# A gather in two halves, three tiled turns in place of four, and loads waited for in groups

## The reference

```python
def reference(x, itok_B_1_198, L0_cond_weights):
    # x: (64, 64, 512) float32; itok: (64,) int32; weights: (200, 64, 64) float32
    w = L0_cond_weights[itok_B_1_198]                    # (64, 64, 64): one 64 x 64 matrix for each sample
    return x + jnp.einsum('bct,bcd->bdt', x, w)
```

## Time and profile before

| | us |
|---|---|
| median of 3 runs | 47.34 (47.32 to 47.43) |
| the profiled execution | 47.17 |
| its span, from the first to the last instruction | 45.3 |
| TensorE busy | 24.1 |
| VectorE busy | 14.8 |
| ScalarE busy | 13.9 |
| moved by DMA | 17.83 MB, mean 394 GB/s |

### The profile page before, as it was taken

One profiled execution on the slowest core, in us unless ns is written; L12 is line 12 of the kernel. 1 busy time (PEld: TensorE's weight loads), 2 busy tenths in 40 slices (PEclk: granted clock), 3 DMA queues, 4 the chain that ended last, 5 costly groups with the idle time before them and its releaser, 6 DMA issues.

```text
span 45.3 us, 305 instructions
## 1 busy us (share of the span) xinstructions
PE 24.1 (53%) x98; PEld 10.0 (22%) x98; DVE 14.8 (33%) x24; ACT 13.9 (31%) x16; POOL 1.6 (4%) x9
## 2 busy tenths in 40 slices
PE   0040000000000099999999999999999999700000
PEld 0040000000000042233454335445344344000000
DVE  1310000000039930067599960280280286140000
ACT  0899100000000050067589840260260265130000
POOL 4009000000000000000000000000000000000000
PEclk9999999999999999999999999999999999999997
DMA  0589999999999999999999999999999999999990
GB/s 0 109 333 434 413 427 427 442 405 434 449 413 427 434 420 427 427 420 427 427 420 427 427 427 420 427 427 420 434 449 391 449 434 413 427 434 384 431 395 22
DMA packets 2594, 17.83 MB, mean 394 GB/s; under 512 B 290, under 2 KB 290, under 8 KB 546
## 3 DMA queue, kind: packets, MB, share of 16 engines
q1 hardware_dynamic: 2448, 16.78, 88.9%
q0 software_dynamic: 144, 1.05, 5.5%
q10 hardware_dynamic: 2, 0.00, 0.0%
HBM read 9.44 MB, written 8.39 MB: 394 GB/s over the span
## 4 chain that ended last, share of the span: by engine, by line
PE 52%; DMA 21%; DVE 7%; issue 5%; POOL 1%; POOLq 1%; DVEq 0%
PE product L148 31%; DMA gathered<-weights,table_row 21%; PE product L152 21%; DVE w_all L179 5%; DVE y_sb L192 2%; POOL piece L124 1%; DVE gathered L176 1%; POOLq L33 1%; DVEq L173 0%; POOLq L201 0%
## 5 line engine op out<-in xcount | busy, mean ns | idle before, releaser
L152 PE MATMUL product<-x_sb,w_all 64*64 64x512 f32 x64 | 9.6, 760 | 12.9 <-DVE w_all L179 12.9
L148 PE MATMUL product<-x_sb,w_diag 128*128 128x512 f32 x32 | 14.0, 595 | 0.0
L188 DVE COPY y_sb<-product 128x1024 f32<-128x1024 f32 x7 | 8.6, 1225 | 11.1 <-PE product L148 6.8
L114 ACT COPY y_sb<-product 128x1024 f32<-128x1024 f32 x7 | 7.1, 1013 | 11.8 <-PE product L148 7.4
L148 PEld LDWEIGHTS product<-x_sb,w_diag 128*128 128x128 f32 x32 | 6.0, 190 | 7.9 <-issue 7.9
L152 PEld LDWEIGHTS product<-x_sb,w_all 64*64 64x64 f32 x64 | 3.5, 209 | 18.3 <-DVE w_all L179 13.0
L110 ACT COPY w_diag<-w_all 64x256 f32<-64x256 f32 x4 | 2.5, 636 | 11.2 <-DVE w_all L179 11.2
L176 DVE TENSOR_TENSOR gathered<-gathered,piece 128x64 f32<-128x64 f32 x1 | 0.3, 270 | 10.0 <-DMA gathered<-weights,table_row 10.0
L179 DVE STREAM_TRANSPOSE w_all<-gathered 128x2048 f32<-128x2048 f32 x1 | 2.3, 2311 | 0.0
L105 ACT COPY w_diag<-zero 64x1024 f32<-64x1024 f32 x2 | 2.1, 1042 | 0.0
L192 DVE COPY y_sb<-product 128x512 f32<-128x512 f32 x2 | 1.4, 692 | 1.5 <-PE product L148 1.5
(11 more groups left out here) (5 smaller groups left out, 0.5 us busy)
## 6 DMA issues: line engine op xcount, KB each, us to landing
x_sb<-x SPq DMA_DIRECT2D x8, 1024.0 KB, 14.1
out<-y_sb SPq DMA_DIRECT2D x7, 1024.0 KB, 6.7
out<-y_sb SPq DMA_DIRECT2D x2, 512.0 KB, 4.9
condition<-conditions ACTq DMA_DIRECT2D x1, 0.2 KB
gathered<-weights,table_row POOLq DMA_INDIRECT x1, 9.7
```

The lines of the kernel that those rows point to most:

```text
L114: nc.scalar.copy(y_sb[:, 4 * turn:4 * turn + 2, :], product[turn % SETS][0][:, :, :]).then_inc(moved_by_act, 1)
L148: product_of = nc.tensor.matmul(product[turn % SETS][j][:, g, :], w_diag[:, n - 4 * TILED, :], x_sb[:, n, :], start=True, stop=True)
L152: product_of = nc.tensor.matmul(product[turn % SETS][h][halves(g), j, :], w_all[halves(h), :, n], x_sb[halves(h), n, :], start=True, stop= ...
L188: nc.vector.tensor_copy(y_sb[:, 4 * turn + 2:4 * turn + 4, :], product[turn % SETS][1][:, :, :]).then_inc(moved_by_dve, 1)
```

## The change

The weight table is given as two tables, one for d below 32 and one for d from 32 on, with rows of 4096 bytes. GpSimd issues two indirect DMAs, each with a semaphore of its own. VectorE waits for the first, adds the identity to its 32 diagonal elements and transposes that half, and then does the same with the second. `w_ready` counts to 2.

The first three turns are tiled in place of the first four, so five turns use `w_diag`, and its zero fill and diagonal copies grow from 16 pairs to 20.

The loads have four semaphores: for turns 0 to 2, 3 and 4, 5 and 6, and 7. TensorE waits for a group at its first turn. The load of turn 2 is issued as two DMAs of two pairs each. SyncE waits for turns 5 and 6 together before the first store.

```diff
--- before.py
+++ after.py
@@ -4,8 +4,10 @@
 
 PAIR = 2
 
-
-def conditioned_residual_kernel(nc: bass.Bass, x: bass.AP, conditions: bass.AP, table: bass.AP, out: bass.AP):
+TILED = 3
+
+
+def conditioned_residual_kernel(nc: bass.Bass, x: bass.AP, conditions: bass.AP, tables: list, out: bass.AP):
@@ -27,7 +29,10 @@
     TURNS = PAIRS // 4
     SETS = 2
     LAST = TURNS - 1
-    TILED = TURNS // 2
+
+    GROUPS = ((0, 1, 2), (3, 4), (5, 6), (7,))
+
+    HALVED = 2
 
     ctx = ExitStack()
     with ctx:
@@ -55,7 +60,7 @@
         product = [[ctx.enter_context(nc.psum_tensor(f"product{s}_{h}", [P, 2, T], fp32)) for h in range(PAIR)]
                    for s in range(SETS)]
 
-        x_loaded = [semaphore(f"x_loaded{turn}") for turn in range(TURNS)]
+        x_loaded = [semaphore(f"x_loaded{turns[0]}") for turns in GROUPS]
         condition_loaded = semaphore("condition_loaded")
         one_set = semaphore("one_set")
         zero_set = semaphore("zero_set")
@@ -63,7 +68,7 @@
         rows_spread = semaphore("rows_spread")
         pieces_set = semaphore("pieces_set")
         rows_known = semaphore("rows_known")
-        w_gathered = semaphore("w_gathered")
+        w_gathered = [semaphore(f"w_gathered{e}") for e in range(K)]
         identity_added = semaphore("identity_added")
         w_ready = semaphore("w_ready")
         multiplied = semaphore("multiplied")
@@ -78,15 +83,20 @@
         def pairs_of(turn):
             return slice(4 * turn, 4 * turn + 4)
 
+        def group_loaded(i):
+            return 16 * sum(2 if turn == HALVED else 1 for turn in GROUPS[i])
+
         def round_of(turn, j):
             return slice(4 * turn + 2 * j, 4 * turn + 2 * j + 2)
 
         @block.sync
         def _(sp):
-            for turn in range(TURNS):
-                sp.dma_start(x_sb[:, pairs_of(turn), :], x[:, pairs_of(turn), :]).then_inc(x_loaded[turn], 16)
-
-            sp.wait_ge(x_loaded[LAST - 1], 16)
+            for i, turns in enumerate(GROUPS):
+                for turn in turns:
+                    for pairs in (round_of(turn, 0), round_of(turn, 1)) if turn == HALVED else (pairs_of(turn),):
+                        sp.dma_start(x_sb[:, pairs, :], x[:, pairs, :]).then_inc(x_loaded[i], 16)
+
+            sp.wait_ge(x_loaded[2], group_loaded(2))
             for turn in range(LAST):
                 sp.wait_ge(moved_by_act, turn + 1)
                 sp.wait_ge(moved_by_dve, turn + 1)
@@ -104,9 +114,9 @@
             for h in range(PAIR):
                 nc.scalar.copy(w_diag[halves(h), :, (1 - h) * D:(2 - h) * D],
                                zero[halves(h), :].unsqueeze(2).to_broadcast([C, PAIRS - 4 * TILED, D]))
-            act.wait_ge(w_ready, 1)
+            act.wait_ge(w_ready, K)
             for turn in range(TURNS):
-                if turn < TILED:
+                if turn < TURNS - TILED:
                     nc.scalar.copy(w_diag[halves(0), pairs_of(turn), 0:D],
                                    w_all[halves(0), :, pairs_of(TILED + turn)].rearrange("p d n -> p n d"))
                 if turn < LAST:
@@ -123,9 +133,11 @@
             for q in range(P // Q):
                 nc.gpsimd.memset(piece[q * Q:(q + 1) * Q, 0:1], float(1 - q % K)).then_inc(pieces_set, 1)
             pool.wait_ge(rows_known, 1)
-            nc.gpsimd.indirect_dma_start(gathered[:, :], None, table,
-                                         bass.IndirectOffsetOnAxis(ap=table_row[:, 0:1], axis=0)
-                                         ).then_inc(w_gathered, 16)
+
+            for e in range(K):
+                nc.gpsimd.indirect_dma_start(gathered[:, e * Q * Q:(e + 1) * Q * Q], None, tables[e],
+                                             bass.IndirectOffsetOnAxis(ap=table_row[:, 0:1], axis=0)
+                                             ).then_inc(w_gathered[e], 16)
 
         @block.tensor
         def _(pe):
@@ -134,9 +146,11 @@
             pe.wait_ge(rows_along, K)
             nc.tensor.matmul(product[0][0][:, 0, 0:1], row_along[:, :, :, :].rearrange("one h k n -> one (h k n)"),
                              one[:, :], start=True, stop=True).then_inc(rows_spread, 1)
-            pe.wait_ge(w_ready, 1)
+            pe.wait_ge(w_ready, K)
             for turn in range(TURNS):
-                pe.wait_ge(x_loaded[turn], 16)
+                for i, turns in enumerate(GROUPS):
+                    if turn == turns[0]:
+                        pe.wait_ge(x_loaded[i], group_loaded(i))
 
                 if turn >= SETS:
                     pe.wait_ge(moved_by_act, turn - SETS + 1)
@@ -170,18 +184,20 @@
             nc.vector.tensor_copy(table_row[:, :], product[0][0][:, 0, 0:1]).then_inc(rows_known, 1)
 
             dve.wait_ge(pieces_set, 2 * (P // Q))
-            dve.wait_ge(w_gathered, 16)
-
-            diagonal = bass.AP(gathered, 0, [[D * Q, P], [Q + 1, Q], [Q * Q, K]])
-            nc.vector.tensor_tensor(diagonal, diagonal, piece[:, :].unsqueeze(1).to_broadcast([P, Q, K]), ALU.add
-                                    ).then_inc(identity_added, 1)
-            dve.wait_ge(identity_added, 1)
-            nc.vector.transpose(w_all[:, :, :], gathered[:, :].rearrange("p (d c) -> p d c", d=D)
-                                ).then_inc(w_ready, 1)
-
-            dve.wait_ge(w_ready, 1)
+            for e in range(K):
+                dve.wait_ge(w_gathered[e], 16)
+
+                diagonal = bass.AP(gathered, e * Q * Q, [[D * Q, P], [Q + 1, Q]])
+                nc.vector.tensor_tensor(diagonal, diagonal, piece[:, e:e + 1].to_broadcast([P, Q]), ALU.add
+                                        ).then_inc(identity_added, 1)
+                dve.wait_ge(identity_added, e + 1)
+                nc.vector.transpose(w_all[:, e * Q:(e + 1) * Q, :],
+                                    gathered[:, e * Q * Q:(e + 1) * Q * Q].rearrange("p (d c) -> p d c", d=Q)
+                                    ).then_inc(w_ready, 1)
+
+            dve.wait_ge(w_ready, K)
             for turn in range(LAST):
-                if turn < TILED:
+                if turn < TURNS - TILED:
                     nc.vector.tensor_copy(w_diag[halves(1), pairs_of(turn), D:PAIR * D],
                                           w_all[halves(1), :, pairs_of(TILED + turn)].rearrange("p d n -> p n d"))
                 dve.wait_ge(multiplied, turn + 1)
@@ -205,18 +221,18 @@
 
     x_laid = np.asarray(x).reshape(B // PAIR, PAIR, C, T).transpose(1, 2, 0, 3).reshape(PAIR * C, B // PAIR, T)
 
-    table = np.asarray(L0_cond_weights).reshape(S, C // Q, Q, D).transpose(0, 1, 3, 2).reshape(S * (C // Q), D * Q)
+    table = np.asarray(L0_cond_weights).reshape(S, C // Q, Q, D // Q, Q).transpose(3, 0, 1, 4, 2).reshape(D // Q, -1, Q * Q)
     arrays = {"x": np.ascontiguousarray(x_laid),
               "conditions": np.ascontiguousarray(np.asarray(itok_B_1_198).reshape(1, B // PAIR, PAIR).transpose(0, 2, 1)),
-              "weights": np.ascontiguousarray(table)}
+              **{f"weights{e}": np.ascontiguousarray(table[e]) for e in range(D // Q)}}
     args = [nc.dram_tensor(name, a.shape, mybir.dt.from_np(a.dtype), kind="ExternalInput").ap()
             for name, a in arrays.items()]
     out = nc.dram_tensor("out", x_laid.shape, mybir.dt.float32, kind="ExternalOutput").ap()
-    conditioned_residual_kernel(nc, *args, out)
+    conditioned_residual_kernel(nc, args[0], args[1], args[2:], out)
     result = run_bass_kernel_spmd(nc, [arrays], core_ids=[0])
 
     laid = np.asarray(result.results[0]["out"])
-    tiled = laid[:, :B // 4].reshape(2, D, B // 16, PAIR, 2, T).transpose(2, 4, 0, 3, 1, 5).reshape(B // 2, D, T)
-
-    whole = laid[:, B // 4:].reshape(PAIR, D, B // 4, T).transpose(2, 0, 1, 3).reshape(B // 2, D, T)
+    tiled = laid[:, :4 * TILED].reshape(2, D, TILED, PAIR, 2, T).transpose(2, 4, 0, 3, 1, 5).reshape(8 * TILED, D, T)
+
+    whole = laid[:, 4 * TILED:].reshape(PAIR, D, B // PAIR - 4 * TILED, T).transpose(2, 0, 1, 3).reshape(B - 8 * TILED, D, T)
     return np.concatenate([tiled, whole])
```

## The result

| | before | changed |
|---|---|---|
| median of 13 runs, us | 47.45 | 48.15 |
| ratio, 95% interval | | 1.0127 [1.0084, 1.017] |
| the profiled execution, us | 47.17 | 48.43 |
| its span, us | 45.3 | 46.2 |

The forecast was 47.44 in a range of 47.2 to 47.95, with "no change" as the likeliest outcome. The kernel is 0.6 us slower by the ratio, and the interval lies clear of 1. The ratio leaves out executions that were disturbed on either side, so it need not be the ratio of the medians.

The account below looks back on a forecast made before the run. The DMA byte stream was taken as the bound, with slack in the matmul chain. 47.17 us plus 0.10 for smaller rows gave 47.27, other terms nothing; on the median's base 47.44, range 47.2 to 47.95.

Parts of the forecast that it names:

- What bounds the kernel: Whole kernel: bytes through the DMA engines set the end, 17.83 MB at 427 GB/s or 41.8 us; the matmul chain has slack.
- The byte stream, +0.10: Gather and turn 2's load, 2.10 MB, in 4096-byte rows at 418 GB/s, not 427: +0.10 us, bounds -0.03 to +0.16.
- The landing of the gather, 13.0: Software queue: part 1 of the gather lands near 13.0 us, bounds 12.8 to 15.5; a late landing decides from about 13.9.
- Add and transpose: Between gather and first matmul: part 1's add 0.22 and transpose 1.2 us, part 0's covered; TensorE starts 1.25 us earlier.
- Three tiled turns: TensorE's turns: one turn changes from tiled to whole, +1.71 us; TensorE ends 0.46 us later, at no cost to the total.
- The slack: Stores on SyncE: the seventh turn's store could be issued 1.3 us later, the last half store 2.1, without delaying the stream.
- the landing notice: Seventh turn's store: time for notice of its landing besides its transfer, estimated at about 0.3 us.
- The rivals: Three other outcomes: TensorE's end decides (47.9, chance 0.07), late gather (0.07 and 0.03), something outside the stream shrinks (47.25, 0.12).
- the second rival: Software queue: part 1 of the gather lands late, TensorE overruns its cover: 49.1 us (chance 0.07) or 52.2 (chance 0.03).
- A fixed cost of each added transfer in the open: Software-generated DMAs: 2.0 us fixed each by the skill page, +4 us if both added transfers paid openly; not used in the sum.

Follow-up runs that it names:

- e11: The changed kernel with four tiled turns in place of three, all else as changed; 48.47 us, ratio 1.0175 to the kernel before.
- e5: The kernel before with the load of turn 4 as two DMAs with rows of 4096 bytes; 47.38 us, ratio 1.0021.
- e3: The kernel before with three tiled turns in place of four, no other edit; 47.85 us, ratio 1.0077.
- e4: The kernel before with the gather as two DMAs of 64 partitions each, rows still 8192 bytes; 51.86 us, ratio 1.0876.
- e18: The changed kernel with the loads of turns 1 and 2 both halved, not turn 2 alone; 48.09 us, ratio 1.0166 to the kernel before.

## Why the prediction was wrong

**What bounds the kernel: right.** The byte stream sets the end before and after. The slices' shares stayed full, the last store still took 4.1 us for 1.23 us of bytes, and giving TensorE 0.9 us back (e11) gained nothing.

**The byte stream, +0.10: wrong, and this is the step that failed.** It measured +0.53 to +0.69. I took the price of 4096-byte rows from the only place that the trace had, the two half stores in the last microseconds, and bounded it with figures of the same place (-0.03 to +0.16). Those are writes, at 42 us; the change puts its small rows into reads at 7 to 13 us, near the start. e5 shows that for reads at 15 us the sum would have been off by little, 0.14 to 0.18 for the 2.10 MB. The bound had no row from the early stretch, and should have been open on that side. The first two microseconds, with 74 GB/s and half-empty slices, could have been taken as a hint that early reads behave otherwise; I had used them only as a fixed offset. What makes the early turn dear stays open.

**The landing of the gather, 13.0: wrong by 1.46.** One against one held, as two windows of the changed kernel's queues show:

```profile
q0 software_dynamic: 53, 0.22, 53.9%
q1 hardware_dynamic: 53, 0.20, 48.0%
```

These are of 9 to 10 us. The lost 0.7 us can account for half of the delay; the rest is not explained. My bounds, 12.8 to 15.5, held it, but it went past the 13.9 from which I had said that a late gather decides. It did not decide (e11), because the stream was late as well.

**Add and transpose: right.** 0.23 and 1.26 against 0.22 and 1.2. Part 0's work ran from 11.7 to 13.2, inside the flight of part 1.

**Three tiled turns: right in length, too sure in effect.** The added whole turn took 3.43 us (17.38 less 13.95), as forecast. All matmuls together took 24.92 us against 23.54, 1.38 more and not 1.71, because the first three turns happened to be 0.38 us quicker. The slack was computed from one execution, and TensorE's first products vary by more than 1 us, so a slack of 1.3 that one trace shows is not there in each run. It was also too large by 0.3: I put 0.3 us for the landing notice, with no row behind it. In the trace of before almost nothing moves from 44.24 us to the landing at 44.87, so the notice takes 0.6 us and the slack was 1.0:

```profile
44.24:44.87 0.63, 0.00 (x0) 0.00 (x0) 0.00 (x0) 0.00 (x0) 0.00 (x0) 0.88 0.02 7
```

By itself the edit costs 0.36 us (e3). In the changed kernel that cost is hidden by the later stream.

**The rivals.** None named the cause. In the second rival the gather lands late and TensorE's end overruns the slack. It did land late, at 14.46, but beside small rows and not beside large ones, and TensorE's end did not decide. A fixed cost of each added transfer in the open, +4 us in the prediction's estimate, is not seen: the whole change cost 0.6. The Trainium skill, "DMA: Bandwidth & Descriptors", section "Bandwidth", has the rule to batch transfers to 1 MiB or more. The runs agree with its sign for the halved load of turn 2 and for the split gather (389 GB/s each), and differ where turn 4 is halved, which cost nothing that the time shows (1.0021).

## What to carry to other kernels

Where the DMA stream is the bound, look at its rate by slices, not at its busy share: the digit of the share stayed at nine while the rate of a slice fell by a third, from 442 to 291 GB/s. Price a smaller row from a row of the trace with the same direction and the same time in the kernel; if there is none, leave the bound open. And a slack no larger than what an engine's pace varies between executions is no cover.

## What was not expected of the hardware

- With the gather as two DMAs into 64 partitions each, and its rows of 8192 bytes unchanged, the whole stream ran at 259 GB/s for 9 us (e4), against about 427.
- A queue's turn to 4096-byte rows between 4 and 8 us lost 0.23 to 0.33 us of the stream (0.46 for the gather's in e18), near 10.5 us nothing clear and at 13 to 18 us about nothing.
- The same 48 tiled products took 7.92, 7.54, 7.17, 6.87 and 6.84 us in five profiles. In the kernel before they went at 5 a microsecond from 16 to 20 us and at 10 from 20 to 24, with the granted clock shown as 1.00 in both; the executions with the quicker products also had the clock at 0.50 (1.2 GHz) earlier at the end.
